# One kernel, one change: a block-diagonal mix of 128 rows becomes two 64-row tiles of the array

## What is computed

```python
att   = softmax(mlp(cond))                                     # 32 x 8
agg_w = einsum('bk,koi->boi', att, weight)                     # one 64 x 64 mix for each batch
y     = einsum('boi,bih->boh', agg_w, x) + (att @ bias_k)[:, :, None]
x     = x + y @ kernel + bias + lora(y)                        # y is 2048 rows of 1024
x     = x + gated_ffn(grouped_conv(x) + ctx)                   # w12, silu, w3
```

## Time and profile before

| | |
|---|---|
| median of 3 runs | 801.6 us (801.58 to 801.7) |
| the profiled execution | 800.24 us |
| its span, first to last instruction | 798.4 us |
| TensorE matmuls, busy | 777.2 us (97% of the span) |
| TensorE weight loads, busy | 655.3 us (82%) |
| VectorE, busy | 526.6 us (66%) |
| ScalarE, busy | 207.0 us (26%) |
| GpSimd, busy | 84.6 us (11%) |
| mean granted TensorE clock | 0.994 |

### The profile page before, as it was taken

How to read it: one execution, slowest core, us unless ns; L and a number is a source line. 1 busy time by engine, 2 the same in 40 slices (tenths; PEclk the granted TensorE clock), 3 DMA queues, 4 the chain that set the end, 5 groups by cost and what they waited for, 6 DMA issues and landing times.

```text
span 798.4 us, 10404 instructions
## 1 busy us (share of the span) xinstructions
PE 777.2 (97%) x3889; PEld 655.3 (82%) x3889; DVE 526.6 (66%) x636; ACT 207.0 (26%) x251; POOL 84.6 (11%) x57
## 2 busy tenths in 40 slices
PE   5998899999999999989999999999999999999998
PEld 4877788888888899968888888888888888888886
DVE  4767676355363469987777759877755896555552
ACT  2531011001000032233333337333333731111110
POOL 4150462422313000000000000000000000000000
PEclk9999899999999999999999999999999999999999
DMA  8967665455484899244445133278862754444441
GB/s 225 286 177 228 170 170 130 127 116 150 111 172 120 182 270 239 81 131 132 131 138 161 43 126 138 80 227 235 240 246 79 261 213 158 160 175 165 158 172 64
DMA packets 88380, 131.47 MB, mean 165 GB/s; under 512 B 11208, under 2 KB 66936, under 8 KB 85656
## 3 DMA queue, kind: packets, MB, share of 16 engines
q1 hardware_dynamic: 85136, 129.90, 55.7%
q10 hardware_dynamic: 3064, 0.90, 0.6%
q0 software_dynamic: 144, 0.21, 0.1%
HBM read 78.20 MB, written 51.72 MB: 163 GB/s over the span
## 4 chain that ended last, share of the span: by engine, by line
PE 85%; SPq 6%; DVE 5%; DMA 4%; issue 1%; ACT 0%; DVEq 0%
PE ps L1836 37%; PE ps L1595 30%; PE ps L1896 18%; SPq L400 2%; DVE cr L1299 1%; DMA raw<-in_L_ffn_kernel 1%; DMA lora_b_scratch<-lb_c_lo 1%; SPq L439 1%; DMA h_f<-h_scratch 1%; SPq L356 1%; DMA lb<-lora_b_scratch 1%; SPq L366 1%; DVE lb_c_lo L1159 1%; DVE w_a_f L1249 1%; DVE wk_lo L1070 0%
## 5 line engine op out<-in xcount | busy, mean ns | idle before, releaser
L1836 PE MATMUL ps<-cr,w_s_hi 128*128 128x512 f32 x512 | 159.0, 392 | 3.4 <-ACT s L921 3.4
L1836 PE MATMUL ps<-cr,w_a_hi 128*128 128x512 f32 x384 | 118.3, 389 | 0.0
L1836 PEld LDWEIGHTS ps<-cr,w_s_hi 128*128 128x128 f32 x512 | 96.6, 189 | 24.5 <-issue 4.5
L1836 PE MATMUL ps<-cr,w_s_lo 128*128 128x512 f32 x256 | 100.1, 391 | 0.0
L1836 PEld LDWEIGHTS ps<-cr,w_a_hi 128*128 128x128 f32 x384 | 71.9, 188 | 14.9 <-issue 0.2
L1595 PE MATMUL ps<-wk_hi,y_hi 128*128 128x512 f32 x256 | 80.5, 395 | 0.0
L1595 PE MATMUL ps<-wk_lo,y_hi 128*128 128x512 f32 x256 | 79.1, 390 | 0.0
L1595 PE MATMUL ps<-wk_hi,y_lo 128*128 128x512 f32 x256 | 78.9, 389 | 0.0
L745 POOL TENSOR_TENSOR x_t<-x_in,f_bias 128x1024 f32<-128x1024 f32 x16 | 63.6, 3981 | 136.9 <-DMA x_scratch<-x_t 136.9
L1147 DVE TENSOR_TENSOR x_t<-ps,x_t 128x1024 f32<-128x1024 f32 x16 | 19.5, 1223 | 88.3 <-PE ps L1595 88.3
L1836 PE MATMUL ps<-cr,w_a_lo 128*128 128x512 f32 x192 | 74.7, 389 | 0.0
(11 more groups left out here) (177 smaller groups left out, 1242.0 us busy)
## 6 DMA issues: line engine op xcount, KB each, us to landing
x_scratch<-x_t SPq DMA_DIRECT2D x128, 64.5 KB, 2.1
x<-x_scratch SPq DMA_DIRECT2D x32, 258.0 KB, 6.9
x_in<-in_x SPq DMA_DIRECT2D x16, 512.0 KB, 6.5
r_scratch<-r_t SPq DMA_DIRECT2D x16, 512.0 KB, 3.2
h_scratch<-s SPq DMA_DIRECT2D x32, 256.0 KB, 2.4
h_f<-h_scratch SPq DMA_DIRECT2D x8, 1024.0 KB, 5.9
res<-r_scratch SPq DMA_DIRECT2D x16, 512.0 KB, 5.1
raw<-in_L_ffn_w SPq DMA_DIRECT2D x56, 128.0 KB, 4.4
```

Of the source, the lines that this page charges most:

```text
L1836: last = pe.matmul(o, l, r, start=first and q == 0 and n == 0, stop=q == 3 and n == 2, skip_group_check=True)
```

## The change

Each batch's mix is used alone. The stationary operand is a block of 64 rows (channels of one batch) by 128 columns (positions); the moving operand is the 64 x 64 mix of that batch. Batch 0 of the tile uses rows 0 to 63 of the array and writes bank 0, batch 1 rows 64 to 127 and bank 1. The zeros beside the blocks are not read any more. The banks now hold one batch each, for all 1024 positions, rather than one half of the positions for both, so the bias, `y_hi` and `y_lo` steps read and write runs of 64 elements rather than 128 or whole rows. Their outputs lie where they lay before. The wait for the bank of tile t - 1 becomes one wait for both banks ahead of the tile, both counts of `y_mm` come with the last block, `first_u` waits for the whole `y_lo` of the tile, and TensorE's loop over i is written out, since a slice of rows of `mix` now has a fixed tile number.

```diff
@@ split_y (ScalarE)
-                    act.activation(y_hi[s][:, a, 4 * h:4 * h + 4, :].rearrange("p k r -> p (k r)"),
-                                   y_f[h][:, :], ACT.Copy).then_inc(y_hi_made, 1)
+                    act.activation(y_hi[s][:, a, :, h * NC:(h + 1) * NC], y_f[h][:, :].rearrange("p (k r) -> p k r", r=NC),
+                                   ACT.Copy).then_inc(y_hi_made, 1)
@@ add_bias, y_rest (VectorE)
-                    dve.tensor_tensor(y_f[h][:, :].rearrange("p (k r) -> p k r", r=P),
-                                      bank(h).rearrange("p (k r) -> p k r", r=P),
-                                      y_bias[:, ds(t * P, P)].unsqueeze(1).to_broadcast([P, 4, P]), ALU.add).then_inc(y_taken, 1)
+                    dve.tensor_tensor(y_f[h][:, :].rearrange("p (k r) -> p k r", r=NC),
+                                      bank(h).rearrange("p (k r) -> p k r", r=NC),
+                                      y_bias[:, ds(t * P + h * NC, NC)].unsqueeze(1).to_broadcast([P, KT, NC]),
+                                      ALU.add).then_inc(y_taken, 1)
...
-                    dve.tensor_tensor(y_lo[s][:, a, 4 * h:4 * h + 4, :].rearrange("p k r -> p (k r)"),
-                                      y_f[h][:, :], y_hi[s][:, a, 4 * h:4 * h + 4, :].rearrange("p k r -> p (k r)"),
-                                      ALU.subtract).then_inc(y_lo_made, 1)
+                    rows = slice(h * NC, (h + 1) * NC)
+                    dve.tensor_tensor(y_lo[s][:, a, :, rows], y_f[h][:, :].rearrange("p (k r) -> p k r", r=NC),
+                                      y_hi[s][:, a, :, rows], ALU.subtract).then_inc(y_lo_made, 1)
@@ y_tile (TensorE)
-                for h in range(2):
-                    if not first:
-                        pe.wait_ge(y_taken, t * 2 + h - 1)
-                    for k in range(4):
-                        c0 = (4 * h + k) * P
-                        last = mm(bank(h)[:, k * P:(k + 1) * P], x_in[slot][:, c0:c0 + P],
-                                  mix[:, ds(t, 1), :].rearrange("p a r -> p (a r)"), True, True)
-                    last.then_inc(y_mm, 1)
+                if not first:
+                    pe.wait_ge(y_taken, t * 2)
+                for k in range(KT):
+                    for b in range(2):
+                        rows, r = slice(b * NC, (b + 1) * NC), slice(k * NC, (k + 1) * NC)
+                        last = mm(bank(b)[:, r], x_in[slot][rows, k * P:(k + 1) * P], mix[rows, t, rows], True, True)
+                        if k == KT - 1:
+                            last.then_inc(y_mm, 1)
@@ first_u
-                pe.wait_ge(y_lo_made, 2 * a + 1 + k // 4)
+                pe.wait_ge(y_lo_made, 2 * a + 2)
@@ the loop of groups
-            with pe.Fori(1, 3) as i:
+            for i in range(1, 3):
```

## The result

The changed kernel takes 807.43 us (median of five runs, 805.25 to 812.85) against 801.7 (801.58 to 801.93, five runs): a ratio of 1.0087, with a 95% interval of 1.0068 to 1.0105. It is slower by 5.7 us where 2.2 were forecast. The profiled execution of each kernel lies at or near its median, so their traces can be set against each other.

What follows compares the result with a forecast made beforehand. The prediction took TensorE to bound the kernel, without a break from 83.55 us on for y tiles 4 to 15. Its terms 4.2 + 0.2 + 0.7 - 2.9 made +2.2 us: 803.8 us, own range 802.0 to 805.6, with rivals 800.6 to 813.0.

Steps and rivals of the forecast that it cites:

- The load sets the pace, and 64 rows load no faster: TensorE's y tiles: each weight load of 128 columns takes 0.112 us, whatever the moving columns, with rows nearly free.
- The faster rival: y tiles: a load into 64 rows takes half, 0.066 us, giving tiles of 1.41 us and 795.0 us in all; chance 0.07.
- The halves load side by side: y tiles: row halves overlap in loads and matmuls as column halves do, so 16 double pairs still take 1.79 us.
- The edges, 0.35 us a tile: y tiles 4 to 15: going to half-arrays and back costs 0.35 us each, 4.2 us for twelve, bounds 2.4 to 6.0.
- The wait for both banks: Ahead of y tiles: free in the loop, hidden for tile 3 by the table wait, 0.7 us of idling before tile 5.
- The 0.7 us before tile 5: TensorE idles there for both VectorE additions on tile 4; booked as +0.7 us, not paid if the clock falls.
- the case that the clock falls: Rival around tile 4: the clock drops despite a shorter wait, so tile 5 finds its additions done; 806.3 us, chance 0.29.
- The start, 0.2 us: Tiles 0 and 1 delay TensorE by up to 0.5 us, mostly covered; 0.2 us booked, bounds 0 to 0.5.
- The clock, -2.9 us: From 83.55 to 89.40 us: the table wait shrinks to about 2.0 us, so the clock stays up, gaining 2.9 us.
- The rival: Around tile 4: the clock falls all the same, partly since its matmuls have half the moving columns; 806.3 us, chance 0.29.
- The sum: Whole kernel: 4.2 edges + 0.2 start + 0.7 tile 5 - 2.9 clock = +2.2 us, giving 803.8 us.
- the clock's fall at 806.3: Rival around tile 4: the clock falls anyway; 4.2 + 0.2 and 0.3 for edges at half rate, +4.7 us; chance 0.29.

Runs made afterwards that it cites:

- the probe: Kernel before with two extra 64-column matmuls on rows 0 to 63 ahead of each y tile from 4 on: 809.73 us; same matmuls on 128 rows: 804.9.
- the 814.54 us run: One of ten further runs of the unaltered changed kernel, the one profiled; the ten had a median of 806.61 us, from 803.73 to 814.54.
- the filled changed kernel: Changed kernel with spare 512-column matmuls in place of TensorE's waits, 8 before tile 3 and 11 before tile 4: 804.44 us, ratio 1.0048.
- `rows_to_5`: Changed kernel's row halves for y tiles 0 to 5 only, the others 128-row matmuls in the changed order: 803.21 us, ratio 1.0034 to before.
- `half_moving`: Kernel before, but from tile 2 on only 64 of the 128 columns of `mix` stream, on all 128 rows: 802.76 us, ratio 1.0018.
- Filled, the kernel before: Kernel before with spare 512-column matmuls in place of TensorE's waits, 8 before tile 3 and 11 before tile 4: 804.6 us, ratio 1.0034.

## Why the prediction was right and wrong

*The load sets the pace, and 64 rows load no faster*: right. A load of 64 rows takes 188 ns at the median, one of 128 rows 192 before, and half the moving columns left the turn at 29.15 us. The faster rival is out. The Trainium skill, TensorEngine Tiling (Array Packing), Theoretical Speedup, promises up to 2 times for a dimension of 64. The prediction read that as half the time of before, and no run shows this: 1.93 us where it was 1.71. Measured against the same 64-row matmuls made one half after the other, 3.32 us, the tiles gain 1.7 times, which agrees with the page. The block-diagonal form already did both batches in one pass, so there was nothing to pack.

*The halves load side by side*: right, by the four loads in 0.30 us, by 0.111 us for each pair of halves, and by 3.32 us a tile when they are made not to. The Trainium skill, TensorEngine Tiling (Array Packing), Key Properties, says that tiles can load and multiply in parallel; for row halves this is what the traces show.

*The edges, 0.35 us a tile*: right. 0.34 by the turn of the loop, 0.33 by the probe. The column halves of the earlier trace rows were good rows to read an unknown row-half edge from. That the agreement is this close is in part luck: of the 0.36 read there, 0.15 lay inside the stretch, and in the y tiles nothing does.

*The wait for both banks*: right that it is free in the loop and in the set-up. The 0.7 us before tile 5 did not come: with the clock low over the LoRA matmuls, TensorE reached tile 5 without a gap, as the prediction had it for the case that the clock falls. Where the clock was up there (the 814.54 us run and the filled changed kernel), that wait was 0.34 us, half of what was booked.

*The start, 0.2 us*: within its bounds of 0 to 0.5. Tiles 0 and 1 delayed nothing (41.25 us to tile 2 against 41.27). The prediction's tile 3 was to end at about 65.4 at full clock; it ran at half clock to 66.9, and VectorE's addition began at 66.92. The wait for the table covered this, but I never asked whether the clock could fall at other places than the one where it already fell, and in the 814.54 us run such a fall cost 6.3 us.

*The clock, -2.9 us*: this is the step that failed, and it failed twice. First, the clock fell all the same, after a wait of 2.48 us, and for 10.3 us in place of 6.9: instead of giving 2.9 us back it cost 1.7 more. The wait was not the 2.0 us of the forecast, since the table came late, but that doesn't save the step: in `rows_to_5` the wait was 1.32 us, and the clock fell for the same 10.3 us. I had taken the length of the wait as the only thing that decides, from two rows that differ in it. Tile 4 after the change has half the moving columns, and `half_moving` shows that fewer columns can bring a fall where there was none. The rival said so and got 0.29 where the forecast got 0.44. Second, the gain would not have lasted. Filled, the kernel before kept the clock up and was slower, since TensorE ran into the z matmuls' wait for `y_lo`; in the 814.54 us run the changed kernel did the same. The cover of that wait was the slow stretch itself, and I priced the clock's gain without asking what is late next. The chain of the earlier trace rows has no gap there, but only because TensorE came late.

*The sum*: 4.1 of edges and about 1.9 in the set-up make 6.0; 5.7 and 5.9 were measured. The measured 807.43 lies outside the forecast's own range of 802.0 to 805.6. It lies inside 800.6 to 813.0 because that range took in the rivals, and it moved the way that was forecast because the edges, and not the clock, decided it. The nearest case was the clock's fall at 806.3. It counted the loss of a gain, but not that the low stretch could grow (1.7 us), nor the late table (2.0 us in the profiled run).

What stays open: why the falls come in one run and not in the next of the same kernel, and how much of the 2.0 us by which the table landed late in the profiled run belongs to the change. `rows_to_5` started tile 4 on time with the same row halves, and the probe of the edge started it at 84.88 without any in the tiles before, which speaks for scatter; no run here took the store and the load of the table apart.

## What to carry to other kernels

When the weight load sets a matmul's pace, removing zeros from the moving side gives nothing, and splitting the rows gives only the edges, here 0.34 us for each trip into half-arrays and back. The probe paid the same for 4 pairs as the changed kernel for 32, so few long stretches should cost less than many short ones; no run here tried that. Alternate the halves if you do split. A stretch at the low clock is not a gain waiting to be had: before booking it, look at what TensorE would meet earlier, and see in a trace whether the clock still stays up once the edit has taken moving columns away.

## What the runs showed of the hardware that was not expected

- Two row halves that take turns load side by side (1.93 us a tile); the same instructions grouped by half do not (3.32 us). The price of the half-arrays, 0.34 us, lies wholly at the two ends of the stretch.
- With half the moving columns the clock fell over a tile where it had stayed at 1.00, though such a tile takes as long at full clock. The mean clock of the runs went from 0.9941 to 0.9913, and for the whole change from 0.9947 to 0.9867, with runs of one kernel from 803.7 to 814.5 us.
- The clock fell to 0.50 for 13.6 us in a stretch in which TensorE was busy throughout, and fell elsewhere after a wait of 1.32 us.
- VectorE's `y_lo`, 1.3 us by itself for the two halves of a tile, took 4.72 us beside a GpSimd addition of 3.83.
